# The last feed forward of a four-layer transformer kernel: its two fp32 products become three fp16 passes each

## The reference, cut to what matters

```python
def _bitlinear(x, w_latent):
    scale = clip(mean(abs(w_latent), axis=1, keepdims=True), 1e-05, None)
    tern = clip(round(w_latent / scale), -1.0, 1.0)
    return x @ ((w_latent + (tern - w_latent)) * scale).T
h = _bitlinear(x, w_fc) + gate * (x @ v.T @ fast_b.T @ u.T)      # 128 -> 512
r = maximum(h, 0.0)
return _bitlinear(r * r, w_proj)                                 # 512 -> 128
```

## Time and profile before

| | us |
|---|---|
| three runs | 1507.51, 1505.87, 1499.92 |
| median | 1505.87 |
| the profiled execution | 1497.63 |
| its span | 1495.7 |
| TensorE busy in it | 1357.8 (91%) |
| VectorE, ScalarE, GpSimd busy | 1038.6, 888.9, 820.1 |
| mean granted clock of TensorE | 0.953 |

### The profile page before, as it was taken

How to read it: one execution, slowest core, us unless ns; L and a number is a source line. 1 busy time by engine, 2 the same in 40 slices (tenths; PEclk the granted TensorE clock), 3 DMA queues, 4 the chain that set the end, 5 groups by cost and what they waited for, 6 DMA issues and landing times.

```text
span 1495.7 us, 37017 instructions
## 1 busy us (share of the span) xinstructions
PE 1357.8 (91%) x14494; PEld 838.4 (56%) x14494; DVE 1038.6 (69%) x2508; ACT 888.9 (59%) x1471; POOL 820.1 (55%) x778
## 2 busy tenths in 40 slices
PE   4799999998979999999978899987978897999988
PEld 3365666665757777777733344433666565444446
DVE  5788888888744344443758989875798476677764
ACT  4487777774759999999834444432233332555542
POOL 6488878776658899989844243212353002434310
PEclk9799999999989999999979999986989899899998
DMA  8000000000013210001101201000000000000000
GB/s 273 5 9 9 9 9 9 2 2 16 30 33 98 61 45 14 28 28 46 33 5 32 65 33 33 30 1 28 1 3 10 0 1 4 5 9 9 2 1 29
DMA packets 25796, 39.62 MB, mean 26 GB/s; under 512 B 7028, under 2 KB 13080, under 8 KB 25144
## 3 DMA queue, kind: packets, MB, share of 16 engines
q1 hardware_dynamic: 25080, 35.58, 7.4%
q0 software_dynamic: 576, 2.10, 0.7%
HBM read 38.72 MB, written 1.05 MB: 27 GB/s over the span
## 4 chain that ended last, share of the span: by engine, by line
PE 67%; DVE 19%; issue 5%; POOL 5%; ACT 3%; DMA 1%; SPq 0%; POOLq 0%; DVEq 0%; ACTq 0%
PE bank L1765 10%; PE bank L1706 10%; PE bank L695 5%; DVE sbuf L834 4%; PE bank L633 4%; PE bank L2231 3%; PE bank L1164 2%; PE bank L649 2%; PE bank L1989 2%; PE bank L1268 2%; POOL sbuf L1118 2%; PE bank L2210 2%; DVE sbuf L851 2%; PE bank L1196 2%; POOL sbuf L1112 2%
## 5 line engine op out<-in xcount | busy, mean ns | idle before, releaser
L1716 ACT ACTIVATE sbuf<-bank,sbuf 128x512 f32<-128x512 f32 (+1 forms) x512 | 323.1, 684 | 30.1 <-PE bank L1706 18.1
L1736 POOL TENSOR_TENSOR sbuf<-sbuf 128x512 f16<-128x512 f32 x256 | 304.9, 1199 | 56.1 <-ACT sbuf L1716 55.1
L310 POOL TENSOR_TENSOR sbuf<-sbuf 128x2 f32<-128x2 f32 (+1 forms) x48 | 39.7, 827 | 353.8 <-DVE sbuf L305 353.8
L1765 PEld LDWEIGHTS bank<-sbuf 128*128 128x128 f16 x3072 | 194.3, 98 | 67.3 <-issue 7.7
L1765 PE MATMUL bank<-sbuf 128*128 128x128 f16 x3072 | 214.6, 220 | 6.3 <-DVEq L1853 6.3
L1706 PE MATMUL bank<-sbuf 128*128 128x512 f16 x768 | 209.2, 382 | 0.0
L834 DVE TENSOR_REDUCE sbuf<-bank 128x4 f32<-128x1024 f32 x128 | 156.3, 1221 | 64.4 <-PE bank L649 51.5
L1848 DVE SCALAR_TENSOR_TENSOR sbuf<-bank,sbuf 128x128 f32<-128x128 f32 x256 | 71.7, 341 | 165.1 <-PE bank L1765 164.9
L1118 POOL TENSOR_TENSOR sbuf<-sbuf 128x512 f16<-128x512 f32 x128 | 148.2, 1179 | 56.8 <-ACT sbuf L1361 56.7
L695 PE MATMUL bank<-sbuf 128*32 128x256 f32 x2048 | 140.3, 393 | 1.6 <-ACT sbuf L782 1.6
L1112 POOL TENSOR_TENSOR sbuf<-sbuf 128x512 f16<-128x512 f32 x96 | 112.0, 1185 | 27.4 <-ACT sbuf L1349 27.1
(11 more groups left out here) (294 smaller groups left out, 2726.8 us busy)
## 6 DMA issues: line engine op xcount, KB each, us to landing
sbuf<-w SPq DMA_DIRECT2D x32, 256.0 KB, 2.9
sbuf<-bias_t SPq DMA_DIRECT2D x4, 1024.0 KB, 11.7
sbuf<-ctx_t SPq DMA_DIRECT2D x24, 128.0 KB, 3.4
sbuf<-bias_q POOLq DMA_DIRECT2D x4, 512.0 KB, 11.6
sbuf<-mask_t SPq DMA_DIRECT2D x8, 256.0 KB, 2.7
sbuf<-bias_t SPq DMA_DIRECT2D x8, 256.0 KB, 3.0
sbuf<-mask_q SPq DMA_DIRECT2D x8, 256.0 KB, 3.7
sbuf<-bias_q SPq DMA_DIRECT2D x8, 256.0 KB, 4.4
```

The costliest lines, as they stand in the source:

```text
L1716: last = act.activation(to, bank[u % 4][:, :], ACT.Gelu, bias=b1[u // U][:, u % FT0:u % FT0 + 1], scale=1 / SCALE)
L1736: g.tensor_tensor(hid16[1][:, u % BUFS, :], hid[:, u % 4, :], hid16[0][:, u % BUFS, :], ALU.subtract)\
L1765: last = pe.matmul(bank[4 + out_no % 2][:, j * P:(j + 1) * P], hid16[h][:, u % BUFS, j * P:(j + 1) * P], w2_16[p][:, w, f * D:(f + 1) * D] ...
```

## The change

Both products of the last feed forward run in three fp16 passes (`PASSES`), on weights scaled by 2^8 so that their low halves keep their bits; the scale is taken out in the relu, the hidden product and the add.

- Weights: `fc16` and `proj16` hold a high and a low half each. In place of one VectorE instruction at unit 26 of the routed stage there are three, and at unit 37 two in place of one.
- Input: `x16` holds two halves of `xn_t`. GpSimd makes them (`halves`: a cast and a subtract for each batch): six batches in the last attention, each behind a norm's power, and the last two in the feed forward itself, between units 6 and 7.
- Hidden: ScalarE runs relu, then the square of it to fp16 (`hid16[0]`); VectorE makes the fp32 product out of the bank and `acted`; GpSimd subtracts the two into `hid16[1]`.
- The down products run LAG = 4 units behind instead of 2, on a ring of 8 (`HIDS`), and a chunk's add comes later.

The core of the diff:

```diff
-            NT, LAG, RING = 4, 2, 4
+            NT, LAG, RING, HIDS = 4, 4, 4, 8
+            SCALE = 2.0 ** 8
+            PASSES = ((0, 0), (0, 1), (1, 0))
...
                 if m == 26:
                     v.wait_ge(s["made_pe"], 3)
-                    v.scalar_tensor_tensor(fc_t, fast, far["gate"][:, 0:1], second[:, :], ALU.mult, ALU.add)\
+                    c.step(v.scalar_tensor_tensor(fast, fast, far["gate"][:, 0:1], second[:, :], ALU.mult, ALU.add)).settle()
+                    c.step(v.tensor_scalar(fc16[:, 0, :], fast, SCALE, None, ALU.mult)).settle()
+                    v.scalar_tensor_tensor(fc16[:, 1, :], fast, SCALE, fc16[:, 0, :], ALU.mult, ALU.subtract)\
                      .then_inc(s["made"], 1)
...
+            def halves(g, k):
+                cols = slice(k * S, (k + 1) * S)
+                g.wait_ge(nrm_xt, nm.ready(k))
+                g.tensor_copy(x16[:, 0, cols], xn_t[:, cols]).then_inc(s["x16"], 1)
+                g.wait_ge(s["x16"], 2 * k + 1)
+                g.tensor_tensor(x16[:, 1, cols], xn_t[:, cols], x16[:, 0, cols], ALU.subtract).then_inc(s["x16"], 1)
...
                     if t == 0:
-                        pe.wait_ge(nrm_xt, nm.ready(2 * c + 1))
+                        pe.wait_ge(s["x16"], 4 * c + 4)
                     if m >= 2:
                         pe.wait_ge(s["hidden"], m - 1)
-                    pe.matmul(bank[INNER[m % 2]][:, :], fc_t[:, t * P:(t + 1) * P], xn_t[:, c * CHUNK:(c + 1) * CHUNK],
-                              start=True, stop=True).then_inc(s["inner"], 1)
+                    for k, (w, xk) in enumerate(PASSES):
+                        last = pe.matmul(bank[INNER[m % 2]][:, :], fc16[:, w, t * P:(t + 1) * P],
+                                         x16[:, xk, c * CHUNK:(c + 1) * CHUNK], start=k == 0, stop=k == 2)
+                    last.then_inc(s["inner"], 1)
...
-                    pe.wait_ge(s["hidden"], m + 1)
+                    pe.wait_ge(s["low"], m + 1)
...
                     for j in range(CT):
-                        last = pe.matmul(bank[DOWNS[c % 2]][:, j * P:(j + 1) * P], hid[:, m % RING, j * P:(j + 1) * P],
-                                         proj_t[:, t, :], start=t == 0 and j == 0, stop=t == NT - 1, skip_group_check=True)
+                        for k, (h, w) in enumerate(PASSES):
+                            last = pe.matmul(bank[DOWNS[c % 2]][:, j * P:(j + 1) * P],
+                                             hid16[h][:, m % HIDS, j * P:(j + 1) * P], proj16[:, w, t * D:(t + 1) * D],
+                                             start=t == j == k == 0, stop=t == NT - 1 and k == 2, skip_group_check=True)
...
-                    wait(act, s["hidden"], m - RING + 1)
-                    act.activation(acted[:, m % RING, :], bank[INNER[m % 2]][:, :], ACT.Relu).then_inc(s["acted"], 1)
+                    wait(act, s["low"], m - RING + 1)
+                    act.activation(acted[:, m % RING, :], bank[INNER[m % 2]][:, :], ACT.Relu, scale=1 / SCALE)\
+                       .then_inc(s["acted"], 1)
+                    act.wait_ge(s["acted"], m + 1)
+                    wait(act, s["down"], m - HIDS + 1)
+                    act.activation(hid16[0][:, m % HIDS, :], acted[:, m % RING, :], ACT.Square).then_inc(s["high"], 1)
...
-                    a = acted[:, m % RING, :]
-                    v.tensor_tensor(hid[:, m % RING, :], a, a, ALU.mult).then_inc(s["hidden"], 1)
-                    if m >= NT and m % NT == LAG:
-                        add(m // NT - 1)
+                    v.scalar_tensor_tensor(hid[:, m % RING, :], bank[INNER[m % 2]][:, :], 1 / SCALE, acted[:, m % RING, :],
+                                           ALU.mult, ALU.mult).then_inc(s["hidden"], 1)
+                    if m >= 2 * NT and m % NT == LAG % NT + 1:
+                        add(m // NT - 2)
...
+            def pool(g):
+                for m in range(len(units)):
+                    if m == TURN_AT + 1:
+                        for k in (B - 2, B - 1):
+                            halves(g, k)
+                    g.wait_ge(s["hidden"], m + 1)
+                    g.wait_ge(s["high"], m + 1)
+                    g.tensor_tensor(hid16[1][:, m % HIDS, :], hid[:, m % RING, :], hid16[0][:, m % HIDS, :], ALU.subtract)\
+                     .then_inc(s["low"], 1)
```

More of the change, by code:

```diff
@@ L494, in ready, with narrow_attention @@
                 eng.wait_ge(g_t, self.base["turned"] + k + 1)
-        def narrow_attention(layer, nm, late, ahead, after, lead=None):
-            gated = lead is not None
+        def narrow_attention(layer, nm, late, ahead, after, lead):
+            gated = layer == 1
             masked = layer == 1
@@ L604, in pool @@
                         after.power(g, b - 2, b - 1)
-                    if gated and b >= 3:
+                    if b >= 3:
                         lead.halves(g, b - 3)
-                if gated:
-                    lead.halves(g, B - 3)
+                lead.halves(g, B - 3)
                 for b in (B - 2, B - 1):
@@ L2358, in gated_feed_forward @@
             return FeedLead(gate, weights, halves, append_programs)
+        EndLead = namedtuple("EndLead", "halves programs")
         def last_feed_forward(nm, tail):
-            s = {k: sem("f3_" + k) for k in ("inner", "acted", "hidden", "down", "made", "made_pe", "stored")}
+            s = {k: sem("f3_" + k) for k in ("inner", "acted", "hidden", "high", "low", "down", "x16", "made", "made_pe", "stored")}
             x0 = x_steps[0] + B
-            NT, LAG, RING = 4, 2, 4
+            NT, LAG, RING, HIDS = 4, 4, 4, 8
+            SCALE = 2.0 ** 8
+            PASSES = ((0, 0), (0, 1), (1, 0))
             units = [(c, t) for c in range(CHUNKS) for t in range(NT)]
             top[0] = 35072
-            fc_t = take([F0])
-            proj_t = take([4, D])
+            fc16 = take([2, F0], F16)
+            proj16 = take([2, F0], F16)
             assert top[0] <= 36800
-            top[0] = 17728
+            top[0] = 29888
+            x16 = take([2, B * S], F16)
+            top[0] = 20800
             fc_e = take([4, D])
@@ L2380, in last_feed_forward @@
             acted = take([RING, CHUNK])
+            top[0] = body
             hid = take([RING, CHUNK])
-            assert top[0] <= 29888
+            hid16 = [take([HIDS, CHUNK], F16) for _ in range(2)]
             INNER, DOWNS, TURNED = (0, 1), (6, 7), 2
@@ L2433, in make_vector @@
             def make_vector(v, m, first, second):
+                c = dve(v)
                 if m == 3:
@@ L2452, in make_vector @@
                     v.wait_ge(s["made_pe"], 4)
-                    v.tensor_copy(proj_t, second[:, :].rearrange("p (t d) -> p t d", d=D)).then_inc(s["made"], 1)
+                    c.step(v.tensor_scalar(proj16[:, 0, :], second[:, :], SCALE, None, ALU.mult)).settle()
+                    v.scalar_tensor_tensor(proj16[:, 1, :], second[:, :], SCALE, proj16[:, 0, :], ALU.mult, ALU.subtract)\
+                     .then_inc(s["made"], 1)
+            def halves(g, k):
[4 more added lines that the diff above has]
+                g.tensor_tensor(x16[:, 1, cols], xn_t[:, cols], x16[:, 0, cols], ALU.subtract).then_inc(s["x16"], 1)
             def tensor(pe):
@@ L2499, in add @@
                     xs = x[:, k * CT:(k + 1) * CT, :]
-                    v.tensor_tensor(xs, bank[DOWNS[k % 2]][:, :].rearrange("p (t d) -> p t d", d=D), xs, ALU.add)\
-                     .then_inc(x_done, 1)
+                    v.scalar_tensor_tensor(xs, bank[DOWNS[k % 2]][:, :].rearrange("p (t d) -> p t d", d=D), 1 / SCALE, xs,
+                                           ALU.mult, ALU.add).then_inc(x_done, 1)
                 for m in range(len(units)):
                     v.wait_ge(s["acted"], m + 1)
-                    wait(v, s["down"], m - RING + 1)
-                    a = acted[:, m % RING, :]
-                    v.tensor_tensor(hid[:, m % RING, :], a, a, ALU.mult).then_inc(s["hidden"], 1)
-                    if m >= NT and m % NT == LAG:
-                        add(m // NT - 1)
-                add(CHUNKS - 1)
+                    wait(v, s["low"], m - RING + 1)
+                    v.scalar_tensor_tensor(hid[:, m % RING, :], bank[INNER[m % 2]][:, :], 1 / SCALE, acted[:, m % RING, :],
+                                           ALU.mult, ALU.mult).then_inc(s["hidden"], 1)
+                    if m >= 2 * NT and m % NT == LAG % NT + 1:
+                        add(m // NT - 2)
+                for k in range(CHUNKS - 2, CHUNKS):
+                    add(k)
+            def pool(g):
[7 more added lines that the diff above has]
+                     .then_inc(s["low"], 1)
             def sync(sp):
@@ L2526, in last_feed_forward @@
             tail["tensor"], tail["vector"] = make, make_vector
-            return append_programs
+            return EndLead(halves, append_programs)
         def retention(nm, ahead, after, lead):
@@ L2826, in sublayers @@
```

(4 more changed lines are left out.)

1 line of the change is left out of this document (added).

## The result

| | median, us | lowest to highest | executions |
|---|---|---|---|
| before | 1504.76 | 1499.92 to 1507.51 | 9 |
| after | 1496.97 | 1491.10 to 1501.05 | 9 |
| ratio after/before | 0.9956 | 0.9934 to 0.9977 (95%) | |
| profiled execution, span | before 1495.7, after 1499.2 | | |

The ratio is 6.6 us off (9.9 to 3.5). It lies just inside the half per cent that was set as "no change", but its interval excludes 1. Two things need explaining. The timed runs gained 2.5 us more than the 4.1 forecast (6.6 by the ratio; the two medians are 7.8 apart). And the two profiled executions, compared with each other, say the opposite: after is 3.5 us longer.

The account below looks back on a forecast made before the run. TensorE alone was taken to bound the last 33 us, at 1.75 us a unit. Terms -5.5 (stage), +0.8 (clock) and +0.6 (attention) summed to -4.1 us: 1501.8 us forecast, range 1495.5 to 1508.5.

Parts of the forecast that it names:

- Pace and walk: Last feed forward: TensorE units fall from 1.75 to 1.32 us; walked through all engines, -5.5 us, bounds 3.2 to 6.8.
- inner 4 waiting for multiply 2: Start of last feed forward: TensorE's inner product 4 waits for VectorE's multiply 2, done at 1466.5, and ends at 1467.8.
- GpSimd's nine lows after the halves: Last feed forward: nine low halves of 1.15 us after the last two batches' halves, ending at 1485.8, together with TensorE.
- The last add: End of last feed forward: the final add near 1487 to 1489 on the old time scale would show the forecast right.
- The square: ScalarE in the last feed forward: new square to fp16 at 0.60 us; with relu and hand-off 1.28 a unit, under 1.32.
- Rival (c): Last feed forward: ScalarE sets the pace at 1.45 us a unit from inner product 4 on, 1503.2 us; chance 0.2.
- The clock term: Start of last feed forward: TensorE's longer idling delays the full clock's return; half of a 1.7 us price, +0.8 us.
- Rival (a): Last feed forward: clock stays low; return at 1488 gives 1510.4 us, none at all 1518.4; chance 0.08.
- Rival (d): Last feed forward: no fall of the clock at all, -6.2 us in sum, 1499.7 us; chance 0.1.
- The attention: Last attention: GpSimd's halves delay VectorE's cuts, 0.5 us in the last batch and about 0.1 after; +0.6, bounds 0 to 4.0.
- Rival (b): Attention and last feed forward: GpSimd and VectorE block one another everywhere, +1.6 us, 1507.5 us; chance 0.12.
- The weights in the routed stage: Routed stage: VectorE's extra weight operations are covered by TensorE's lag of a unit; cost 0, without the cover 0.8 us once.

Follow-up runs that it names:

- lag run: Changed kernel with the down products two units behind the inner ones instead of four; norm scale to end of span 30.4 us, where the walk gave 30.6.
- moved halves: Changed kernel with batch 6's halves made earlier by GpSimd in the attention and batch 7's by ScalarE and VectorE; last stage 26.87 us instead of 27.0.
- one-pass run: Changed kernel with only the highs' pass of three in both products of the last stage, halves still made; last stage 25.45 us.
- the run that forced it: Changed kernel with unused bf16 products filling TensorE's waits, ten before the last attention batch's outputs and four before the stage's third unit; last stage 26.2 us.
- the halves alone: Kernel before with the six pairs of halves on GpSimd in the last attention, results unused, fp32 feed forward kept; last two powers 16.90 us apart.
- the moved one: Kernel before with five repeated VectorE statistics instructions ahead of the last batch's statistics before the routed stage, to shift later work 1.2 us; routed stretch 45.2 us.

## Why the prediction was right, and where it was off

**Pace and walk: mechanism right, term 0.9 too small.** The steps came as walked: 0.65 and 0.67 in the chain, inner 4 waiting for multiply 2, GpSimd's nine lows after the halves arriving together with TensorE. The lag run (30.4 against 30.6), the moved halves and the one-pass run confirm the structure. The term was -5.5 and measured -6.4, with a low stretch of 6.8 us in both traces. The difference is in small sizes: on the time scale of before (9.9 us less) the clock is back at 1467.0, not 1467.7, the nine lows end at 1485.0 and not 1485.8, and the span ends at 1489.3 and not 1490.2. The nine lows ran in 10.1 us, 1.12 each, not 1.15. The last add started at 1486.0 on that scale, just ahead of the 1487 to 1489 that were named as a sign.

**The square.** No row had squared from SBUF; it took 0.630 where the copy from a bank gave 0.60. With the relu and the hand-offs that is some 1.27 a unit, under 1.32. Rival (c), 1.45 a unit, falls.

**The clock term: wrong.** +0.8 was taken for a later return; it returned 0.6 us earlier relative to the norm scale. (The return of before was read as 1467.7; the row gives 1467.6.) The extra idle time of TensorE before inner 2 and inner 4 did not prolong the fall. Rival (a) falls with it. By its own formula a return at 1488 would cost 10.1 and none at all 18.1, each 0.7 more than its sums used; no chance hangs on that. Rival (d), no fall, did not happen by itself, and the run that forced it was worth 0.8 in the new stage. The prediction had it at 1.3.

**The attention: right.** 0.5 in the last batch and nothing in the others. It is 0.37 by the cut at L842, which was forecast at 0.5, and 0.11 by the sixth pair on the next cut, forecast at 0.1: together 0.5 for 0.6. Rival (b), everything blocked, falls: 16.90 with the halves alone, and lows at 1166 ns. The run with two SBUF inputs shows what the disturbance would have cost in the stage had the multiply read the SBUF twice, 5.5 us.

**The weights in the routed stage: right.** The distance of the powers around the first making is 22.56 before (1221.51 to 1244.07) and 22.58 after (1229.72 to 1252.30).

**The sum.** Forecast -4.1. The parts in the traces give -5.9, the timed ratio -6.6 (-9.9 to -3.5). What was off is the walk, by 0.9, and the clock term, which should have been 0 in place of +0.8. That the timed gain comes so near the parts is in part luck: the new kernel's nine executions have 153 us of low time on average and the old one's 12 later ones 158, which by itself would be some 2.4 us (an estimate, half of the difference), and nothing in the forecast foresaw it. The forecast time of 1501.8 is further off, because it started from the median of three runs, 1505.87, and nine gave 1504.76; the median of after, 1496.97, is in the range of 1495.5 to 1508.5.

**What the prediction did not see.** It treated the clock only inside the last stage. Both kernels spend 140 to 172 us in low clock in an execution, in stretches whose place differs between the traces, and this goes with the spread of its times: of the old kernel's 12 later executions the fastest (1502.34) had 144 us of low time, the slowest (1509.82) 172. The new kernel's seven traces without the products in the routed stage all had the long form of the routed stretch. The four of the old one had the short one, counting the moved one with its 45.2. That looks systematic. What stands against it as an effect on the time: three of the new kernel's nine timed executions had a span of 1489.3 to 1491.6 and only 140 to 143 us of low time, against 152 to 162 in the others; and the old one's 12 later executions had 144 to 172 us, 158 on average, against 141 and 140 in its two traces. So the traces of the old kernel are not like its timed executions, and it looks like more than chance: the unchanged old kernel was run singly five times (1497.63, 1496.65, 1499.86, 1498.20, 1499.79 us), and each is under the lowest of both its timed series (1499.92 and 1502.34), while single executions of the new one (1501.05, 1496.85) are not below its series. **Open** is why that is so, and why traces of one kernel fall in one form so regularly and those of the other in the other form; the timed executions have no rows by which to see it, and moving the work by about 1 us did not turn the form over. With it stays open how much of the timed 6.6 us is the stage and how much is clock elsewhere.

## What to carry to other kernels

Three fp16 passes in place of an fp32 product gain at most the difference in TensorE's own time, here 0.43 us a unit: walk the stage through all engines, since the lows, the halves and the lag decide how much arrives, and read one operand of the multiply from the bank when GpSimd works beside it. Don't take the difference of two profiled spans for the effect of a change: here it was +3.5 us where the timed runs gained 6.6, while the new kernel's stage alone repeated to 0.02 us. Compare stretch by stretch, with the granted clock beside each.

## What the hardware showed

- Twenty useless bf16 products in two waits of TensorE made the old kernel 0.8% faster (0.9921), more than the change under study. The low time fell from 158 to 130 us with them. Behind the same two waits, 2.9 and 3.3 us, the routed stretch had 10.2 us of low clock in one trace and 27.3 in another, and was 7.5 us longer for it.
- Less work can also mean a lower clock: with one pass of three, TensorE had 0.57 of its clock for most of the stage.
- A VectorE multiply with two SBUF inputs and GpSimd's subtraction lengthened one another by 0.28 and 0.26 us on average (0.69 and 1.17 undisturbed), neither by the other's whole duration.
